# A conv block kernel on one Trainium2 core: slot 0 by itself at the start of the slot pipeline, other groups at its end, and context sums in two parts

## What is computed

```
x = x + L0(gn(x))   # 32x32 mixes over height per width position, relu, batch norm over (batch, width, channel)
x = x + L1(gn(x))   # three two-layer silu MLPs of 64 channels, a product over one spatial index
                    # per channel (bikh,bkjh->bijh), two residual MLPs, times self, an output MLP
x = x + L2(gn(x))   # 3-tap conv along height; (row sum + column sum - y)/sqrt(H+W-2), relu
x = x + L3(gn(x))   # 64 -> q, ctx, 4 gates; three depthwise convs (3x3, 5x5, 7x7) with gelu, each gated
                    # and added; gelu of the mean over the image (global context) times gate 3, added;
                    # 64x64, times q, layer norm over channels, 64x64
```

## Time and profile before

| | |
|---|---|
| device time, 3 runs | median 973.38 us (969.78 to 977.17) |
| profiled execution | 977.0 us, span 975.0 us |
| busy in the span | TensorE 856.8 us (88%), VectorE 673.1 (69%), ScalarE 483.5 (50%), GpSimd 214.6 (22%) |
| chain that ended last | TensorE 75%, VectorE 13%, ScalarE 5%, issue 4% |
| mean granted clock of TensorE | 0.949 |
| stages (us from the start) | L0 to 99; slot pipeline 99 to 589; convs 590 to 804; tail from 815 |

### The profile page before, as it was taken

The page is one execution under the profiler, slowest core; times in us unless marked ns, Lnnn a source line. Parts: engine busy times, 40 slices in busy tenths (PEclk is TensorE's granted clock), DMA queues, the critical chain, the costliest instruction groups (busy, mean ns, idle before and its releaser), DMA issues.

```text
span 975.0 us, 23006 instructions
## 1 busy us (share of the span) xinstructions
PE 856.8 (88%) x9473; PEld 599.2 (61%) x9473; DVE 673.1 (69%) x1000; ACT 483.5 (50%) x615; POOL 214.6 (22%) x159
## 2 busy tenths in 40 slices
PE   5896268989998899999987788999999986999997
PEld 2664224444544444444455568999999983777775
DVE  5888864666888777877887642555556655777776
ACT  3675865765675656665643123222222223555554
POOL 2000260222222222222232000000000005766660
PEclk9999577989999999999999889999999998999999
DMA  9824002233333333211121111333333310111112
GB/s 191 175 38 49 7 7 83 107 129 122 113 121 129 125 105 137 89 25 25 25 49 24 24 66 60 108 125 130 115 113 130 130 65 1 43 65 54 54 61 69
DMA packets 48312, 80.07 MB, mean 82 GB/s; under 512 B 15328, under 2 KB 24672, under 8 KB 47200
## 3 DMA queue, kind: packets, MB, share of 16 engines
q1 hardware_dynamic: 43104, 69.86, 23.6%
q10 hardware_dynamic: 5120, 8.92, 3.7%
HBM read 59.90 MB, written 35.19 MB: 98 GB/s over the span
## 4 chain that ended last, share of the span: by engine, by line
PE 75%; DVE 13%; ACT 5%; issue 4%; POOL 1%; DMA 1%; ACTq 1%; SPq 0%; DVEq 0%; POOLq 0%
PE ps L1254 71%; PE ps L1633 1%; PE ps L1625 1%; DVE WK L960 1%; DVE st L972 1%; DVE WK L889 1%; DVE RG L1121 1%; PE ps L1359 1%; ACT WK L561 1%; DMA XB<-in_x_dram 1%; DVE RG L1015 1%; ACT WK L631 1%; ACT WK L584 0%; ACTq L697 0%; ACT WK L617 0%
## 5 line engine op out<-in xcount | busy, mean ns | idle before, releaser
L1254 PE MATMUL ps<-WK,RG 128*128 128x256 f32 (+2 forms) x1280 | 241.8, 386 | 10.2 <-DVE WK L889 5.0
L1254 PEld LDWEIGHTS ps<-WK,RG 128*128 128x128 f32 (+1 forms) x1280 | 226.0, 265 | 25.7 <-issue 10.6
L1254 PE MATMUL ps<-WK,WT 64*64 64x512 f32 (+2 forms) x1216 | 185.7, 628 | 9.9 <-ACT WK L631 4.6
L631 ACT ACTIVATE WK<-ps,BC 128x1024 f32<-128x1024 f32 x96 | 105.7, 1116 | 88.7 <-PE ps L1254 79.8
L1254 PE MATMUL ps<-RG,WT 64*64 64x512 f32 (+1 forms) x832 | 140.4, 642 | 9.7 <-DVE RG L1015 5.1
L741 ACT ACTIVATE WK<-ps 128x1024 f32<-128x1024 f32 x48 | 49.2, 1024 | 164.5 <-PE ps L1254 164.5
L1254 PEld LDWEIGHTS ps<-WK,WT 64*64 64x64 f32 (+1 forms) x1216 | 56.4, 144 | 107.5 <-issue 83.4
L631 ACT ACTIVATE RG<-ps,BC 128x1024 f32<-128x1024 f32 x96 | 105.7, 1119 | 24.5 <-PE ps L1254 24.3
L1254 PEld LDWEIGHTS ps<-WK 32*32 32x32 f32 (+2 forms) x4352 | 73.0, 145 | 54.0 <-issue 44.7
L1254 PE MATMUL ps<-WK 32*32 32x32 f32 (+2 forms) x4352 | 87.9, 237 | 18.8 <-issue 14.9
L539 POOL TENSOR_TENSOR RG<-WK,gates 128x512 f32 (+1 forms) x32 | 42.4, 1324 | 247.3 <-ACT WK L749 238.2
(11 more groups left out here) (187 smaller groups left out, 1246.7 us busy)
## 6 DMA issues: line engine op xcount, KB each, us to landing
band_rows<-band_tables SPq DMA_DIRECT2D x64, 192.0 KB
band_rows<-band_tables SPq DMA_DIRECT2D x32, 384.0 KB
RG<-band_rows SPq DMA_DIRECT2D x16, 768.0 KB, 4.3
RG<-band_rows SPq DMA_DIRECT2D x8, 1536.0 KB, 6.5
WK<-WK ACTq DMA_DIRECT2D x64, 136.0 KB
XB<-in_x_dram SPq DMA_DIRECT2D x32, 256.0 KB, 12.4
out_dram<-WK SPq DMA_DIRECT2D x64, 128.0 KB, 2.1
band_tables<-sums SPq DMA_DIRECT2D x8, 94.5 KB
```

What stands on the lines that cost most here:

```text
L631: nc.scalar.activation(dst, unit(pair(job, s)), ACT.Silu, bias=BC[:, bias:bias + 1]).then_inc(out_of(job, s)[0], 1)
L1254: return nc.tensor.matmul(out, lhsT, rhs, start=start, stop=stop)
```

## The change

1. The first norm's sets are NORM1: slot 0; slots 1 to 3; then fours as before. In front of the ticks only slots 0 to 3 are batch-normed and added, and only slot 0 is turned, measured and normalised. Slots 1 to 3 arrive in tick 0, slots 4 to 7 in tick 1, slots 8 and 9 in tick 2. Batch norm of slots 8 to 15 stands in ScalarE's list behind the evictions of tick 0, and ScalarE's silu of left2(0) behind that.
2. All sixteen adds are VectorE's: slots 4 to 7 in its tick 1, slots 8 to 15 at the end of its tick 2. GpSimd's four copies into SPREAD move in front of the power of the batch norm.
3. VectorE takes the arriving slots' stats behind times_self, in place of in front of turn_l.
4. The last norm's sets are NORM3: fours, then slots 12 to 14, then slot 15. The set of three is done inside the ticks: values, factors and three norms in VectorE's tick 21 in front of add_x3(15); its c3 on TensorE in front of spread(15). Slot 15's c3 follows behind the ticks.
5. The context sums are made in two parts: columns up to LATE = 896 (all but the last block of channels), which wait for the reduces of seven blocks, and the last 128. Each part has its matmuls and its gelus; gelu writes GLOB after the gate of step (0, 7) rather than after all gates.

```
-POOL_X1 = (2, 6, 8, 10, 12, 14)
+NORM3 = (*(range(GS * g, GS * (g + 1)) for g in range(NG - 1)), range(NS - GS, NS - 1), range(NS - 1, NS))
+NORM1 = (range(0, 1), range(1, GS), *(range(GS * g, GS * (g + 1)) for g in range(1, NG)))
+LATE = (C - UCH) * NS
 def arriving(t):
-    return range(GS, 2 * GS) if t == 0 else range(2 * GS + t - 1, min(2 * GS + t, NS)) if t > 0 else range(0)
+    first = (1, GS, 2 * GS)
+    return range(first[t], first[t + 1]) if t < 2 else range(2 * GS + t - 1 - (t == 2), min(2 * GS + t, NS))
...
@@ GpSimd: the four copies into SPREAD, then the power of the batch norm, then
-            residual1([i for i in POOL_X1 if i < NS // 2])
             norm1_pow(0)
-            residual1([i for i in POOL_X1 if i >= NS // 2])
+            norm1_pow(1)
...
@@ ScalarE
-            batch_norm(range(0, NS // 2))
-            for i in (1, 3):
-                to_channels(i)
-            batch_norm(range(NS // 2, NS))
+            batch_norm(range(0, GS))
+            to_channels(0)
+            batch_norm(range(GS, NS // 2))
...
                 for i in arriving(u):
-                    to_channels(i)
+                    if i != 2:
+                        to_channels(i)
+                if u == 0:
+                    batch_norm(range(NS // 2, NS))
...
-            act.wait_ge(sem("glob_mm"), 1)
-            act.wait_ge(sem("gated"), NSTEP)
-            for j in range(2):
-                nc.scalar.activation(GLOB[:, 1024 * j:1024 * (j + 1)], unit(j), ACT.Gelu, scale=1.0 / TOK
-                                     ).then_inc(sem("glob_out"), 1)
+            act.wait_ge(sem("gated"), ORDER.index((0, NU - 1)) + 1)
+            for n, c in enumerate((slice(0, LATE), slice(LATE, 1024))):
+                act.wait_ge(sem("glob_mm"), n + 1)
+                for bh in range(BH):
+                    nc.scalar.activation(GLOB[:, 1024 * bh:1024 * (bh + 1)][:, c], unit(2 * n + bh)[:, c], ACT.Gelu, scale=1.0 / TOK
+                                         ).then_inc(sem("glob_out"), 1)
...
@@ VectorE
-            residual1(range(0, NS // 2))
-            for i in (0, 2):
-                to_channels(i)
+            residual1(range(0, GS))
             stats1(0)
             factors1(0)
             for t in range(TICKS + 2):
+                if t == 1:
+                    residual1(range(GS, NS // 2))
+                    to_channels(2)
+                    stats1(1)
+                    factors1(1)
                 tick(t, (residual0, 4), (slot_stats3, 7))
-                if t >= 10 and (t - 10) % GS == 0 and t < 10 + GS * NG:
+                if t >= 10 and (t - 10) % GS == 0 and t < 10 + GS * (NG - 1):
                     stats3((t - 10) // GS)
...
-                if u == 0:
-                    residual1(range(NS // 2, NS))
-                for i in arriving(u - 1):
-                    dve.wait_ge(*out_of("xt", i))
-                    slot_stats(st, i, "bn1")
-                    if i % GS == GS - 1:
-                        group_stats(i // GS, st, "bn1", me1, "stats1_ready")
...
                 tick(t, (edges, 6), (turn_l, 2), (turn_k, 2), (residual_1, 4), (stats2, 5), (moments2, 5),
-                     (times_self, 4), (factors2, 5), (add_x3, 6), (norm1, 0))
-            factors3(NG - 1)
-            for i in range(NS - GS, NS):
-                norm3(i)
+                     (times_self, 4))
+                if t == TICKS:
+                    stats3(NG - 1)
+                    factors3(NG - 1)
+                    for i in NORM3[NG - 1]:
+                        norm3(i)
+                for i in arriving(1) if u == 1 else arriving(u - 1) if u > 2 else ():
+                    dve.wait_ge(*out_of("xt", i))
+                    slot_stats(st, i, "bn1")
+                    if i % GS == GS - 1:
+                        group_stats(NORM1[i // GS + 1], st, "bn1", me1, "stats1_ready")
+                tick(t, (factors2, 5), (add_x3, 6), (norm1, 0))
+                if u == 0:
+                    residual1(range(NS // 2, NS))
+            stats3(NG)
+            factors3(NG)
+            norm3(NS - 1)
             for i in range(NS - GS, NS):
                 project_out(i)
...
@@ TensorE
             def spread(s):
+                if s == NS - 1:
+                    c3(NG - 1)
                 pe.wait_ge(*out_of("t", s))
...
-            for i in range(GS):
-                to_channels(i)
+            to_channels(0)
             c1(0)
...
-                tick(t, (left2, 1), (m1b, 3), (m0a, 2), (self2, 1), (times, 5), (right1, 0), ...
+                tick(t, (left2, 1), (m1b, 3), (m0a, 2), (self2, 1), (times, 5))
+                if t == 1:
+                    c1(1)
+                tick(t, (right1, 0), (m0b, 2), (left1, 0), ...
...
-            pe.wait_ge(sem("rsum_ready"), BH * NU)
-            for j in range(4):
-                last = mm(ps[:, j, :], ones[:, :], RSUM[:, HALF * j:HALF * (j + 1)])
-            last.then_inc(sem("glob_mm"), 1)
-            pe.wait_ge(sem("glob_out"), 2)
+            for n, parts in enumerate((((0, 512), (512, LATE)), ((LATE, 1024),))):
+                pe.wait_ge(sem("rsum_ready"), BH * (NU - 1 + n))
+                for bh in range(BH):
+                    for a, b in parts:
+                        last = mm(unit(2 * n + bh)[:, a:b], ones[:, :], RSUM[:, 1024 * bh + a:1024 * bh + b])
+                last.then_inc(sem("glob_mm"), 1)
+            pe.wait_ge(sem("glob_out"), 2 * BH)
```

More of the change, by code:

```diff
@@ L117, in psum_jobs @@
         for job, lag in TICK:
+            if (job, t) == ("l1", 1):
+                yield "c1", 1
             if 0 <= t - lag < NS:
@@ L121, in psum_jobs @@
             yield "c3", (t - GROUP3) // GS
+        if t == TICKS - 1:
+            yield "c3", NG - 1
         if t % GS == GS - 2 and t < NS - GS:
-            yield "c1", t // GS + 1
+            yield "c1", t // GS + 2
         for i in arriving(t):
@@ L128, in psum_jobs @@
             yield "pj1", i
-    yield "c3", NG - 1
+    yield "c3", NG
     for i in range(NS - GS, NS):
@@ L274, in conv_preact_kernel @@
         ROWH = GFL[:, 392:784].bitcast(BF16).rearrange("p (a n) -> p a n", a=2)
-        X1_P = [len([k for k in range(i + 1) if k in POOL_X1]) for i in range(NS)]
-        X1_D = [i + 1 - X1_P[i] for i in range(NS)]
         HI = [WK[:, 16384 + TOK * i:16384 + TOK * (i + 1)] for i in range(8)]
@@ L973, in slot_stats, with group_stats, group_factors @@
                                        ).then_inc(sem(done), 1)
-            def group_stats(g, stats, done, to, ready):
-                dve.wait_ge(sem(done), 2 * GS * (g + 1))
-                for j in range(GS):
-                    ins = nc.vector.bn_aggr(mv[:, j, :], stats[:, j, :])
+            def group_stats(slots, stats, done, to, ready):
+                dve.wait_ge(sem(done), 2 * slots.stop)
+                for j in slots:
+                    ins = nc.vector.bn_aggr(mv[:, j % GS, :], stats[:, j % GS, :])
                 link(ins)
-                c = slice(GS * g, GS * (g + 1))
-                link(cp(to[:, 0, c], mv[:, :, 0]))
+                c, m = slice(slots.start, slots.stop), mv[:, slots.start % GS:(slots.stop - 1) % GS + 1, :]
+                link(cp(to[:, 0, c], m[:, :, 0]))
                 link(TT(to[:, 1, c], to[:, 0, c], to[:, 0, c], ALU.mult))
-                TT(to[:, 1, c], to[:, 1, c], mv[:, :, 1], ALU.add).then_inc(sem(ready), 1)
-            def group_factors(job, g, gmv, var):
+                TT(to[:, 1, c], to[:, 1, c], m[:, :, 1], ALU.add).then_inc(sem(ready), 1)
+            def group_factors(job, g, slots, gmv, var):
                 dve.wait_ge(sem(job + "_mm"), g + 1)
-                c = slice(GS * g, GS * (g + 1))
-                cp(gmv[:, 0:2, c], ps[:, 2 * pair(job, g), 0:2 * GS].rearrange("p (a s) -> p a s", a=2)
+                c, n = slice(slots.start, slots.stop), len(slots)
+                cp(gmv[:, 0:2, c], ps[:, 2 * pair(job, g), 0:2 * n].rearrange("p (a s) -> p a s", a=2)
                    ).then_inc(out_of(job, g)[0], 1)
@@ L1110, in norm3 @@
             def norm3(s):
-                dve.wait_ge(sem("gnrstd4"), s // GS + 1)
+                dve.wait_ge(sem("gnrstd4"), 1 + [s in g for g in NORM3].index(True))
                 if s < 3 or s == NS - GS:
@@ L1527, in _ @@
             for t in range(TICKS):
-                tick(t, (left2, 1), (m1b, 3), (m0a, 2), (self2, 1), (times, 5), (right1, 0), (m0b, 2), (left1, 0),
-                     (third0, 5), (third1, 5), (third2, 5), (co, 4), (spread, 5), (oa, 3), (self1, 0), (right2, 0),
+                tick(t, (left2, 1), (m1b, 3), (m0a, 2), (self2, 1), (times, 5))
+                if t == 1:
+                    c1(1)
+                tick(t, (right1, 0), (m0b, 2), (left1, 0), (third0, 5), (third1, 5), (third2, 5), (co, 4), (spread, 5), (oa, 3), (self1, 0), (right2, 0),
                      (ob, 3), (ein0, 1), (ein1, 1), (m1a, 2), (ein2, 1), (ein3, 1))
```

102 lines of the change are left out of this document (45 added, 57 removed).

## The result

The changed kernel has a median of 968.23 us over 20 runs (961.97 to 973.02), against 973.62 us (969.08 to 982.03, 20 runs) for the kernel before on the same chip. The ratio of the two is 0.993 with a 95% interval of 0.9908 to 0.9952: **about 6.8 us faster, and the interval lies within 1%**. The two medians by themselves are 5.4 us apart. The profiled execution of the changed kernel took 972.1 us, with a span of 970.1.

The account below looks back on a forecast made before the run. TensorE was taken to bound the kernel (busy 856.8 of 975.0 us), leaving its standing places to gain; front -3.5, end -0.7 and context -2.8 sum to -7.0, 966.4 us on the median, own range 962.5 to 971.

Parts of the forecast that it names:

- front, replay: Front, replayed with row durations: first layer 15.1 us earlier, of which 3.9 to 4.6 us is kept; 4.3 taken.
- copies beside setup: Front: GpSimd's SPREAD copies beside VectorE's setup steps cost 0.8 us, bounds 0 and 6.0.
- end: End of the slot pipeline: one stall of 3.62 us becomes 2.1 and 2.2; sum -0.7, bounds -1.5 and +2.7.
- +1.0: End of the pipeline: project(12) starts at 578.8 instead of 577.82, behind two stalls.
- -1.7: End of the pipeline: stretch at clock 0.50 (578.9 to 582.3) would be 1.7 us shorter at the upper level.
- sums: Context: GpSimd starts the tail at 812.3 instead of 815.12, -2.8 us; bounds 0 to -3.0.
- The stats behind times_self are free: Later ticks: stats behind times_self cost nothing, because norm1 has most of a tick to spare.
- The price that I had worked out from the rule: Front: copies hold VectorE up by most of 6.0 us; front about +1.0 instead of -3.5, time 970.9.
- The shorter stalls don't lose the level: End of the pipeline: granted clock assumed to stay up behind the stalls of 2.1 and 2.2 us.
- slower by the clock: Rival: low granted clock throughout ticks 1 to 3 costs about 11 us; +4, 977.4; chance 0.08.
- More at the front: Rival: TensorE's holes (2.06, 1.45) in tick 1 fall into existing waits, copies cost nothing; -11.3, 962.1; chance 0.25.
- The front gives nothing: Rival: stall on batch norm 8 to 15 and serial adds eat the lead; -3.5, 969.9; 0.17 with nothing from sums.

Follow-up runs that it names:

- e2: Kernel before with only the new sets of the last norm (slots 12 to 14, then 15): 973.42 us, ratio 1.0002.
- e3: Kernel before with only the context sums in two parts: 971.41 us, ratio 0.9996.
- e10: Changed kernel run once more, unaltered: 967.65 us, ratio 0.9922 to the kernel before.
- e1: Front part alone: changed kernel with last norm and context sums as in the kernel before; 968.96 us, ratio 0.9946.
- e4: Reordered end: changed kernel with norms of slots 12 to 14 behind add_x3(15) and slot 15's stats, slot 15's values before the evictions; 964.82 us, ratio 0.991.
- e6: Changed kernel with reordered end, GpSimd's four copies into SPREAD moved back behind the power of slots 1 to 3: 963.87 us, ratio 0.9887.
- e9: Kernel before with only the arriving slots' stats moved behind times_self on VectorE: 971.45 us, ratio 0.9969.

## Why the prediction was right, and where it was not

Forecast: 966.4 against a median of 973.4, that is -7.0; measured -6.8 by the ratio (interval -9.0 to -4.7) and, the second time, -7.6. The median, 968.23, is 1.8 us above the forecast. Each term by its stage is a mean over the kernels with and without the part. Without the front part those are three (before, e2, e3), with it five (after, e10, e1, e4, e6); the end without its part is before, e3, e9 (e1, 31.2, has another middle in front of it) and with it e2, after, e10. The setup before the first batch norm is in no row.

| step | forecast | measured |
|---|---|---|
| front, replay | -4.3 | 78.6 to 75.1: **-3.6** |
| copies beside setup | +0.8 | 0 |
| ticks 1 to 5 (statistics behind times_self) | 0 | 112.2 to 109.3: **-2.9** (-3.3 without low stretches, of which the statistics are 2) |
| ticks 6 to 15, and to times(15) | 0 | 227.6 to 228.0, 38.3 to 39.4: +1.5 |
| end | +1.0 - 1.7 = -0.7 | 31.5 to 32.3: **+0.8** |
| sums | -2.8 | 224.8 to 222.0: **-2.8** |
| sum | -7.0 | -7.0 |

That the sums agree to the tenth is luck: the terms for the end and for ticks 1 to 5 were off by 1.5 and 2.9 us, with opposite signs, and ticks 6 to 15 and the stretch behind add 1.5 that vary as much from one execution to the next.

**The front replay held, step by step.** Norm of slot 0 at 111.06 (forecast 110.9 to 111.7), first layer 112.02 (111.9), norm of slot 1 128.61 (129.1), TensorE behind the silu of left2(0) at 133.28 (133.4), adds 137.83 to 147.0 (137.7 to 147.2), evictions from 145.87 (145.1, behind the products, as counted), turn_m(0) done at 148.16 (148.4), where it holds TensorE up by 0.56 us, left2(2)'s silu at 171.97 (171.3), oa(0) at 176.88 (176.2). The oa(0) row is 3.9 us earlier between the two profiled executions, although the first batch norm began 1.0 later (100.24 against 99.25); counted from the batch norm it is -4.9, and -3.6 by the means of the stages, since the one profile that I worked from has a front 1.6 us above the mean of 78.6: 80.3, longer than in the two other executions with the same code (78.0 and 77.7).

**The copies were mis-sized**: I had taken 0.8 from adds that ran beside copies of 1.50 us. The copies take 0.60 here, and the step behind them waits for ScalarE anyway. The Trainium skill's rule that I weighed (SBUF — State Buffer, "Who interferes with whom": a GpSimd instruction and a VectorE one on the shared ports exclude each other) would have had most of 6 us of holding up. The trace agrees in that some operations beside a copy are stretched, by 0.17 us in the row above, and that a norm beside GpSimd adds takes 2.83. The price that I had worked out from the rule is not borne out: none of it reached the path.

**"The stats behind times_self are free" failed.** I had only looked at who waits for the statistics (norm1, with most of a tick to spare), not at who stood behind them: turn_l and times_self, on which TensorE's products and the layer oa wait. In the kernel before, ticks 1 to 5 without low stretches go from a mean of 108.8 to 106.9. In the kernel with the front part they are 104.5 to 106.4. That the order is a cause, worth 2 us of ticks 1 to 5, is shown by the two experiments that move nothing else (108.8 to 106.9, and 107.5 to 105.5). The other 1.2 us or so that the front part takes off ticks 1 to 5 have no experiment, and neither is it shown which of TensorE's waits ends sooner. The word "free" was wrong in the front as well, where late statistics cost 2.7 us; in the changed kernel the two nearly cancel.

**"The shorter stalls don't lose the level" failed.** Most of the +1.0 came (+0.8), and the two stalls stood where the forecast had put them (2.1 and 2.2 forecast, 1.82 and 1.90 found). The -1.7 did not come at all: 3.41 us at the level 0.50 lie behind the second stall, as many as behind the one of 3.62. The reordered end shows what the part is worth without them: 27.8 against 31.5, -3.7.

**The sums held in both ways**: the size, and the next wait (VectorE's last gate-and-add, 807.76 and 2.29, then GpSimd at 810.13).

**Of the rivals**, slower by the clock didn't come: low stretches in the front cost 19.4 us before and 17.5 after. "More at the front" (-11.3) had the copies right, and the first hole did shrink (1.20 us at 142.42, where it was 2.06), but the front gained no more than the replay; the unforeseen gain lies behind it. "The front gives nothing" (-3.5) named the two costs rightly (batch norm 3.4, adds 1.1 or more), neither ate the lead, and -3.5 lies outside the interval of both timings.

**Open**: why the ticks take about 2.5 us more at full clock in the two kernels that reach times_self(0) sooner by the split batch norm or by GpSimd's adds (108.3 and 108.2), and not in the ones with early statistics (105.0 and 106.1). No run tells this.

## What to carry to other kernels

When a set of small operations is moved in an engine's list, ask for each instruction that it is moved past who waits behind it: the same part of the change cost 0.8 us with its norms in front of one add, and gave 3.7 with them and the last statistics in a better order. Removing a stall pays twice if the clock falls behind it, but two stalls of half its length can still lose the level, so count only on the gain that is left if they do. Where a profile names an engine for a wait, check that the wait needs that engine's last step: a semaphore that every add raises named the adds here, while the transposes held up the evictions. With a timing that resolves 3 us and single traces whose middle moves by 10, judge a part of 1 to 3 us by the duration of its own stage in several kernels that share it, not by where an execution stands later on.

## What the runs showed of the hardware

- **The granted clock is not settled by the length of one stall.** It stayed at 1.00 behind 1.82 us without work at 567.0 and fell to 0.50 behind 1.90 us at 573.6, 4.8 us of work later; behind a stall of 1.02 it stayed at 1.00. All three executions with the two stalls and all seven with the one of 0.60 to 1.02 show the same. Whether the two stalls count together was not tried apart.
- **Ticks 6 to 15 take 222.5 to 232.6 us** in fourteen executions, whose kernels differ there by no more than the place of the statistics, and the low stretches in them cost 4.7 to 14.5 us; without these it is 217.8 to 222.1. The changed kernel itself took 231.3 and 228.8. Over all the ticks from 1 to 15 the low stretches come at a few places (near 30, 100, 130, 200, 225, 310 and 340 us behind the first times_self), and each execution has another choice of them: the changed kernel had 0.91 at 200 to 220, in its ticks 1 and 2 (1.8 us of loss, in the row further up), where its clock was 1.00 on both sides. An execution's position in the middle therefore says little on a change of a few us.
- **A GpSimd add stretches only some of VectorE's work.** Beside four of them (2.5 us each) a norm took 2.83 and another 2.49, against 0.81 alone, while the transposes between them took 1.98 and 1.22, as always (1.95 and 1.25 in the changed kernel). The GpSimd copies took 0.60 beside VectorE's setup in the changed kernel and 0.95 to 1.50 at 134 to 139 us in the kernel before, mostly beside VectorE's adds.
